# Attention and expert feed-forward on one core: softmax denominators of pairs 8 to 28 from one sum of eight tiles, and two moved VectorE steps

## The reference

```python
attn = jnp.einsum('bhnd,bhsd->bhns', q, k) * scale      # scale = 64 ** -0.5
attn = jnp.clip(attn, -11.0, 11.0)
attn = jax.nn.softmax(attn, axis=-1)                    # over the 1024 context rows
out = jnp.einsum('bhns,bhsd->bhnd', attn, v)
out = out.transpose(0, 2, 1, 3).reshape(b, n, INNER)
return out @ Wo + bo
...
sel = jax.nn.sigmoid(jnp.einsum('bsd,ed->bse', input_tensor, expert_sel))
scores = jax.nn.relu(jnp.einsum('bsd,edh->bseh', input_tensor, keys))
out = jnp.einsum('bseh,ehv,bse->bsv', scores, values, sel)
```

## Time and profile before

| | |
|---|---|
| median of 3 runs | 1008.09 us (1007.96 to 1010.86) |
| profiled execution, its own time | 1009.1 us |
| its span, first to last instruction | 1007.3 us |
| TensorE busy | 978.5 us, 97% |
| VectorE busy | 809.4 us, 80% |
| ScalarE busy | 532.1 us, 53% |
| DMA share of 16 engines | 32.4% |

### The profile page before, as it was taken

The page is one execution under the profiler, slowest core; times in us unless marked ns, Lnnn a source line. Parts: engine busy times, 40 slices in busy tenths (PEclk is TensorE's granted clock), DMA queues, the critical chain, the costliest instruction groups (busy, mean ns, idle before and its releaser), DMA issues. The chain is left out here.

```text
span 1007.3 us, 16017 instructions
## 1 busy us (share of the span) xinstructions
PE 978.5 (97%) x5712; PEld 621.8 (62%) x5712; DVE 809.4 (80%) x1275; ACT 532.1 (53%) x765; POOL 146.5 (15%) x130
## 2 busy tenths in 40 slices
PE   4999999999999999999999999998999989999998
PEld 3755555555555555555555555554555468888898
DVE  7888999999899989998889888988889876545322
ACT  3666666666566656565656555555555542222221
POOL 3200000000000000000000000320000144445443
PEclk9999999999999999999999999999999999999999
DMA  7343333323232333233322223232222471242331
GB/s 215 114 133 96 112 92 112 120 75 91 74 90 74 93 89 104 75 96 84 96 80 86 64 85 84 84 85 84 85 64 66 136 272 61 109 127 85 125 105 42
DMA packets 68601, 99.84 MB, mean 99 GB/s; under 512 B 21872, under 2 KB 44656, under 8 KB 66480
## 3 DMA queue, kind: packets, MB, share of 16 engines
q1 hardware_dynamic: 68528, 98.89, 32.4%
HBM read 70.01 MB, written 10.75 MB: 80 GB/s over the span
## 5 line engine op out<-in xcount | busy, mean ns | idle before, releaser
L1130 ACT ACTIVATE wide_a<-score_ps 128x1024 f32<-128x1024 f32 x256 | 248.8, 1026 | 118.2 <-PE score_ps L886 118.0
L1433 DVE TENSOR_SCALAR wide_a<-wide_a 128x1024 f32<-128x1024 f32 x256 | 169.9, 691 | 44.1 <-ACT wide_a L1130 44.0
L1442 DVE TENSOR_TENSOR p_sum<-wide_a 128x1024 f32<-128x1024 f32 x128 | 158.0, 1234 | 2.3
L899 PE MATMUL o_ps<-wide_a,v_sb 128*64 128x512 f32 x512 | 124.0, 605 | 0.8 <-issue 0.8
L899 PE MATMUL o_ps<-wide_a,values_a 128*64 128x512 f32 x512 | 124.0, 605 | 0.2 <-issue 0.2
L886 PEld LDWEIGHTS score_ps<-q_hi,k_hi 64*128 64x128 f32 x512 | 47.9, 183 | 111.4 <-issue 77.5
L886 PE MATMUL score_ps<-q_hi,k_hi 64*128 64x512 f32 x512 | 114.6, 444 | 1.7 <-DVE k_lo L1426 0.9
L1961 DVE SCALAR_TENSOR_TENSOR act<-h_ps,wide_a 128x512 f32<-128x512 f32 x62 | 42.8, 690 | 87.5 <-PE h_ps L152 82.1
L1885 ACT CAST act_hi<-act 128x512 fp32r<-128x512 f32 x64 | 39.8, 621 | 138.4 <-DVE act L1961 138.4
L886 PE MATMUL score_ps<-q_hi,k_lo 64*128 64x512 f32 x512 | 101.0, 391 | 0.0
L886 PE MATMUL score_ps<-q_lo,k_hi 64*128 64x512 f32 x512 | 100.5, 389 | 0.0
(11 more groups left out here) (225 smaller groups left out, 1929.6 us busy)
## 6 DMA issues: line engine op xcount, KB each, us to landing
wide_a<-sel_dram SPq DMA_DIRECT2D x16, 1024.0 KB, 4.6
k_swap<-k SPq DMA_DIRECT2D x124, 128.0 KB, 2.3
w_hi<-packs_hi SPq DMA_DIRECT2D x26, 384.0 KB, 3.0
w_lo<-packs_lo SPq DMA_DIRECT2D x26, 384.0 KB, 3.6
den<-inv_dram SPq DMA_DIRECT2D x64, 128.0 KB, 2.8
ctx_raw<-ctx SPq DMA_DIRECT2D x24, 128.0 KB, 2.2
packs_hi<-w_hi SPq DMA_DIRECT2D x8, 384.0 KB, 3.0
packs_lo<-w_lo SPq DMA_DIRECT2D x8, 384.0 KB, 3.6
```

The costliest lines, as they stand in the source:

```text
L899: mm = pe.matmul(o_ps[DH * h:DH * h + DH, :], v_sb[n // 2 % 2][:, at:at + DH], probs[s % RING][:, h, :], start=(s == 0), stop=(s == STEPS ...
L1130: act.activation(probs[s % RING][:], score_ps[s % 2][:], ACT.Exp, scale=DH ** -0.5).then_inc(exp_done, 1)
L1433: dve.tensor_scalar(probs[s % RING][:], probs[s % RING][:], CLIP_HI, CLIP_LO, ALU.min, ALU.max).then_inc(clipped, 1)
L1442: dve.tensor_tensor(p_sum[m][:], first, second, ALU.add).then_inc(summed_up, 1)
```

## The change

Three things, all in the attention.

1. For n in `EIGHTS` (8 to 28, 21 pairs) VectorE makes one sum of all eight tiles. `sum_quad(n, 0)` stays; new is `sum_six(n)`, which adds `p_sum[1]` into `p_sum[2]` at the end of macro step 3; `sum_all(n)` adds `p_sum[2]` into `p_sum[3]` where `sum_quad(n, 1)` stood. TensorE's four matmuls with ones then take 256 columns each instead of 512, head h and query half e at partition 64h+32e. ScalarE copies 256 columns of `den`, each turning DMA moves half, and VectorE inverts without adding first.
2. The output remainder `split_o(n-2)` of pairs 9 to 28 moves from behind `sum_up` and `stats` in macro step 0 to directly behind the first two clips.
3. `normalize` of the context tile (n below 22) moves from ahead of clip 2 to behind it.

```diff
--- before.py
+++ after.py
@@ -50,6 +50,7 @@
 CLIP_LO = 1.670170079024566e-05
 
 FIRST_TILES = 10
+EIGHTS = range(PAIRS, NPAIR - 3)
 FIRST_DUOS = FIRST_TILES // 2
 MACROS = STEPS // 2
 QUAD = 32
@@ -191,16 +192,23 @@
     for h in range(2):
         for e in range(2):
             at = DH * h + QUAD * e
-            row = sh.den[at:at + 1, :].rearrange("a (p j) -> a p j", p=DH)
-            sp.dma_start(sh.den_rows[DH * h:DH * h + DH, e, :], row).then_inc(sh.den_turned, DMA)
+            if n in EIGHTS:
+                row = sh.den[at:at + 1, 0:NQ // 2].rearrange("a (p j) -> a p j", p=QUAD)
+                sp.dma_start(sh.den_rows[at:at + QUAD, 0, :], row).then_inc(sh.den_turned, DMA)
+            else:
+                row = sh.den[at:at + 1, :].rearrange("a (p j) -> a p j", p=DH)
+                sp.dma_start(sh.den_rows[DH * h:DH * h + DH, e, :], row).then_inc(sh.den_turned, DMA)
 
 
 def invert_den(dve, sh, n):
 
     wait(dve, sh.den_turned, 4 * DMA * (n + 1))
     wait(dve, sh.inv_stored, DMA * n)
+    if n in EIGHTS:
+        dve.reciprocal(sh.inv_rows[:], sh.den_rows[:, 0, :]).then_inc(sh.den_inv, 1)
+        return
     dve.tensor_tensor(sh.inv_rows[:], sh.den_rows[:, 0, :], sh.den_rows[:, 1, :], ALU.add).then_inc(sh.den_added, 1)
-    wait(dve, sh.den_added, n + 1)
+    wait(dve, sh.den_added, n + 1 - sum(1 for i in EIGHTS if i < n))
     dve.reciprocal(sh.inv_rows[:], sh.inv_rows[:]).then_inc(sh.den_inv, 1)
 
 
@@ -508,7 +516,7 @@
 
         def quads(n):
 
-            return sum(1 if i in THREE_PARTS else 2 for i in range(min(n, NPAIR - 2) + 1))
+            return sum(1 if i in THREE_PARTS else 3 if i in EIGHTS else 2 for i in range(min(n, NPAIR - 2) + 1))
 
         def k_half(t, half):
 
@@ -916,7 +924,13 @@
                 pe.wait_ge(ones_ready, 1)
                 wait(pe, den_evac, n)
                 wait(pe, y_added, 2 * (n - 1) - (1 if n >= NPAIR - 2 else 0))
-                if n == NPAIR - 1:
+                if n in EIGHTS:
+                    for e in range(2):
+                        for h in range(2):
+                            at, half = DH * h + QUAD * e, slice(e * (NQ // 2), (e + 1) * (NQ // 2))
+                            mm = pe.matmul(side_ps[at:at + QUAD, 0:NQ // 2], ones[:], p_sum[3][:, h, half],
+                                           start=True, stop=True)
+                elif n == NPAIR - 1:
                     mm = ones_round([(0, p_sum[2]), (1, p_sum[3])], False, True)
                 elif n in THREE_PARTS:
                     ones_round([(0, p_sum[1])], True, False)
@@ -1138,7 +1152,8 @@
                 act.wait_ge(den_ready, n + 1)
 
                 wait(act, o_scaled, n)
-                act.copy(den[:], side_ps[:]).then_inc(den_evac, 1)
+                width = NQ // 2 if n in EIGHTS else NQ
+                act.copy(den[:, 0:width], side_ps[:, 0:width]).then_inc(den_evac, 1)
 
             def round_weights(w):
 
@@ -1447,6 +1462,17 @@
                 first, second = p_sum[2 * half], p_sum[2 * half + 1]
                 dve.tensor_tensor(second[:], first[:], second[:], ALU.add).then_inc(quads_up, 1)
 
+            def sum_six(n):
+
+                dve.wait_ge(quads_up, quads(n) - 2)
+                dve.wait_ge(summed_up, MACROS * n + 4)
+                dve.tensor_tensor(p_sum[2][:], p_sum[1][:], p_sum[2][:], ALU.add).then_inc(quads_up, 1)
+
+            def sum_all(n):
+
+                dve.wait_ge(quads_up, quads(n) - 1)
+                dve.tensor_tensor(p_sum[3][:], p_sum[2][:], p_sum[3][:], ALU.add).then_inc(quads_up, 1)
+
             dve.wait_ge(power_ready, 3)
             stats_first(0)
             stats_first(1)
@@ -1515,14 +1541,14 @@
                 p, t = n + 1, n + FIRST_TILES
                 for m in range(MACROS):
                     last = n == NPAIR - 1
-                    if m == 1 and t < TILES:
-                        wait(dve, turned, t - FIRST_TILES)
-                        normalize(t, ctx_n[:], x_n[:])
                     if m == 3 and n in (24, 25):
                         head_rows(2 * (n - 24))
                     if m == 3 and n in (26, 27):
                         head_split_x(2 * (n - 26))
                     clip(n, 2 * m)
+                    if m == 1 and t < TILES:
+                        wait(dve, turned, t - FIRST_TILES)
+                        normalize(t, ctx_n[:], x_n[:])
                     if n == 0 and m == 0:
                         rope_first_cos(1)
                     if m == 1 and p < NPAIR:
@@ -1532,12 +1558,15 @@
                         scale_o(dve, sh, n - 1)
                     if n == 0 and m == 0:
                         rope_first_sin(1)
-                    if m == 0 and n >= NPAIR - 3:
+                    if m == 0 and n > PAIRS:
                         split_o(dve, sh, n - 2, n % 2)
                     if m == 0 and n >= 3:
                         add_y(dve, sh, n - 3, 1, job_ps[1] if last else side_ps, bo)
                     if m == 0 and n > 0 and n - 1 not in THREE_PARTS:
-                        sum_quad(n - 1, 1)
+                        if n - 1 in EIGHTS:
+                            sum_all(n - 1)
+                        else:
+                            sum_quad(n - 1, 1)
                     if m == 2 and n >= 2:
                         add_y(dve, sh, n - 2, 0, side_ps, bo)
                     sum_up(n, m)
@@ -1548,7 +1577,7 @@
                             stats(t)
                         if n == 0:
                             split_v_weights(1)
-                        if 2 <= n < NPAIR - 3:
+                        if 2 <= n <= PAIRS:
                             split_o(dve, sh, n - 2, n % 2)
                         if n == 29:
                             invert_gate(dve, sh, 0, 0)
@@ -1574,6 +1603,8 @@
                         add_y(dve, sh, n - 2, 1, job_ps[0], bo)
                         split_o(dve, sh, n - 1, 0)
                         split_keys(3)
+                    if m == 3 and n in EIGHTS:
+                        sum_six(n)
                     if m == 3:
                         if t < TILES:
                             split_tile(t)
```

## The result

The changed kernel takes **1015.88 us** (median of 4 runs, 1014.43 to 1016.45); the kernel before took 1009.05 beside it (4 runs). The ratio is 1.0072, with a 95% interval from 1.0046 to 1.0098. It is slower by some 7 us where I had forecast 6.8 us faster, and the time lies outside my range. The profiled execution took 1014.43 us, its span 1012.6, against 1007.3 before.

A forecast was written before the change was run, and what follows sets the result against it. TensorE, busy 97% of the span, was taken as the bound. Narrow blocks gain 9.0 us, less 1.2 of stalls and 1.0 in pair 27: 6.8 us, so 1008.1 to 1001.3 us, range 998.6 to 1005.3.

The forecast's parts named there:

- The matmuls with ones: TensorE's block with ones at half width: 1.00 to 0.57 us, 0.43 per pair, 9.0 us over 21 pairs.
- The rule that I weighed: Narrow weight loads set the block's pace: 0.87 us, a gain of 0.13 each; as a rival 1006.4 us, chance 6%.
- What VectorE gets: VectorE's extra 128x1024 sum, 1.14 us, less the half-sums' addition, 0.19: net 0.95 us per pair, 20 us in all.
- my sign of 0.6: Rival 1 decides where more than 0.6 us of VectorE idle stays in a pair with x rows.
- rival 1: VectorE becomes the bound, the ring of waits not opened: pairs last 25.3 or 25.0 us, kernel 1028 us; chance 6%.
- The ring: ScalarE and VectorE wait for each other before exponential 2; early `o_lo` opens it, clip 2 at 334.0 instead of 334.75.
- The deadline: TensorE's ones need `sum_all` 7.14 us into a pair; odd pairs 9 to 21 stall about 1.2 us in all.
- At nothing, the DMAs: Turning DMAs, still four with half the bytes, cost nothing: hidden behind the inverse, which VectorE comes to only later.
- `normalize` for pairs 0 to 7: Moving the normalizing there was put at nothing, since TensorE's few waits are not on it.
- From pair 22 on: No tile is left to normalize, so VectorE keeps more of the idle time it is given back; no size given.
- Pair 27, late by 1.0 us: The last sum, 0.79 us ahead of the ones before, gets 1.74 more and makes TensorE wait about 1.0 us.
- Rival 2: TensorE waits for `sum_all` in nearly every pair, 0.1 to 0.4 us; half the 9.0 goes: 1004.5 us; chance 14%.

The follow-up runs named there:

- free_narrow: Kernel before with the narrow block with ones in pairs 8 to 28, no extra VectorE sum (tiles 0 to 3 left out of denominators): 999.54 us, ratio 0.9929.
- after_swap: Changed kernel with the sum of the first four tiles' pairs put ahead of the scaling of o_raw: 1006.81 us, ratio 0.9993.
- norm_only: Kernel before with only `normalize` moved behind clip 2, in all pairs that have a tile: ratio 1.0039.
- olo_only: Kernel before with only the output remainder `split_o` early in pairs 9 to 28: ratio 1.0021.
- sums_only: Kernel before with the sums of eight and narrow blocks in pairs 8 to 28, but neither move: 1017.38 us, ratio 1.0087.
- single mends: Changed kernel with one repair: old normalizing place up to pair 8 (1.0027), `split_o` behind the last sum (1.0016), or sums of eight only to pair 23 (1.003).
- three_mends: Changed kernel with normalizing in its old place up to pair 8, sums of eight only to pair 23, `split_o` behind the last sum: 1008.94 us, ratio 1.0003.
- olo_behind_sum: Changed kernel with the output remainder `split_o` directly behind the last sum of eight instead of ahead of it: ratio 1.0016.
- the exchange: Sum of the first four tiles' pairs put ahead of the scaling of o_raw; made alone in the kernel before: 1005.99 us, ratio 0.9971.
- mends_swap: `three_mends` with the sum of the first four tiles' pairs put ahead of the scaling of o_raw: 999.21 us, ratio 0.9908.
- before_swap: Kernel before with only the sum of the first four tiles' pairs put ahead of the scaling of o_raw: 1005.99 us, ratio 0.9971.
- sums_to_23: Changed kernel with one sum of eight only for pairs 8 to 23; pairs 24 to 28 sum in fours again: ratio 1.003.
- norm_late_pairs: Changed kernel with the normalizing back ahead of clip 2 in pairs 0 to 8: ratio 1.0027.

## Why the prediction was wrong

- **The matmuls with ones, 0.43 us each: right.** 1.00 to 0.57 us, 0.42 per pair in `free_narrow`. All eight loads of a block start within 0.1 us. The line of the narrow block in pair 12 (ns of one, then the first and last start in us):

```profile
L931 PEld LDWEIGHTS side_ps<-p_sum,ones x8: 106/108/109, 334.9 to 335.0; 128*32 128x32 f32 x8
L931 PE MATMUL side_ps<-p_sum,ones x8: 379/391/403, 334.9 to 335.2; 128*32 128x256 f32 x8
```

The rule that I weighed (the Trainium skill, TensorEngine Tiling, section Restrictions: column tiling disables fast weight load) gives no time; 0.87 was my estimate, eight loads of 108 ns one after another. The trace, with 0.57, shows that the loads don't set the pace here.

- **What VectorE gets, 0.95 us per pair: right** (345.34 to 359.47 us over 16 pairs is 0.88). In pair 12 it is busy for 23.02 us, less than the 23.31 that I had, which is why its 0.89 us of idle there, over my sign of 0.6 for rival 1, did no harm.
- **The ring is opened: right.** Clip 2 is at 337.58, 9.78 us into pair 12; I had said 9.8.
- **The deadline, 1.2 us of stalls in pairs 9 to 21: wrong, and the central fault.** They were 4.3. I had the last sum of pair 13 at 7.05 us into the pair (it ended at 7.0) and that of pair 11 at 7.6 or 7.7 (7.8). But I took three pairs as the sample, and let even pairs recover 1.1 us. Pair 12 ended at 6.8, not 6.0, and pairs 14, 18 and 20 at 7.2 to 7.7. ("Three lie as late as 11" was misread as well: before the change the last sum ended at 5.96 us in pair 11, 5.88 in 15 and at most 5.62 in the other odd ones.) The margin of 0.1 us was below the size of what VectorE waits for behind DMAs: 2.9 us in 8 waits for `den`, all in pairs 9 to 20, and 4.5 in 5 for `k_swap`, of which 1.3 lie ahead of pair 22. Six of the eight stalls (pairs 11, 15, 17, 19, 20, 21) have a wait for `den` in the pair before them; the wait of 1.07 us for `k_swap` in pair 13 stands ahead of that of 14. In `after_swap`, where the last sum no longer waits for `den`, it ends in pairs 11, 17 and 19 at 7.0 to 7.1 instead of 7.4 to 7.9. Over pairs 9 to 24 of the changed kernel:

```profile
DVE wide_a L1448 <- ACT wide_a L1144: 12.9, 16, 1.9
DVE k L1409 <- DMA k_swap<-k: 4.5, 5, 1.6
DVE o_raw L233 <- DMA den<-inv_dram: 2.9, 8, 0.5
```

- **At nothing, the DMAs, "hidden behind the inverse, which VectorE comes to only later": only half looked at.** Halving the turning DMAs cost nothing, but the DMAs that follow the inverse were hidden by idle time that I was spending in the same text; no term stood for them. One such wait stands late in pair 18, two sums ahead of the last sum, which falls in pair 19; there TensorE waits 0.76 us ahead of the ones:

```profile
494.29 0.69 DVE L233 TENSOR_TENSOR o_raw<-o_raw,den 128x512 f32<-128x512 f32 x1 [0.51 <-DMA den<-inv_dram]
494.89 1.22 DVE L1463 TENSOR_TENSOR p_sum<-p_sum 128x1024 f32<-128x1024 f32 x1
```

- **At nothing, "`normalize` for pairs 0 to 7": wrong, 3.5 us.** The cover that I named (TensorE's few waits are not on it) was never checked against the late `o_lo` of these pairs. A step that moves from inside a wait to behind it is new work on the path there; its price was 0.3 to 0.6 us a pair in pairs 4 to 6 and nothing in 7 and 8, where there was room. In pair 3 it was 1.8, because the inverse came later as well and VectorE waited 1.23 us for `den` in pair 2: the same DMA that I had put at nothing.
- **From pair 22 on, "VectorE keeps more of what it is given back": wrong for 25 and 26, 4.6 us.** No tile is normalized there, but the head statistics and the new sum stand together ahead of the last sum, and the clock falls behind one of the two waits (pair 26).
- **Pair 27, late by 1.0 us:** TensorE waited 2.74 us ahead of the block. The pair still came out 0.5 us shorter, against the 0.6 longer that I had (1.0 less a block), but that is luck: the stall of 2.75 us at the key projection stands in the profile of the kernel before and in none of the 17 others. Against kernels without the extra sum (25.3 us in `norm_only`, 25.6 in `olo_only`) pair 27 is 2.5 to 2.9 us longer.

```profile
703.34 0.84 PE L931 MATMUL side_ps<-p_sum,ones 128*32 128x256 f32 x8 [2.74 <-DVE p_sum L1474]
```

Set against my sum of 6.8, by stage: pairs 2 to 8 took 3.5 us; pairs 9 to 24 gave 1.9 where I had 6.9 - 1.2, 3.8 short (3.1 of it in waits); pairs 25 and 26 took 4.6 where two blocks were to give 0.86, 5.5 short; pair 27 was better than forecast by 1.1; all after it fell short by 0.4. That is 12.1, and 6.8 - 12.1 is -5.3, the span's 5.3 us. Rival 2, which named waits in nearly every pair, had the mechanism, but with a floor at half the gain. No rival had the other stages, and rival 1 (VectorE as the bound, the ring not opened) did not occur here: VectorE still idles 1.1 us in pair 11. It is `sums_only`, without the moves, that shows its ring.

What stays open: why the late DMA comes when it does, and how much of each cause there is in the time, since the single mends take 4 to 6 us each from the changed kernel, 14 in all, and together (`three_mends`) only 7. It was not tried to make the inverse's chain itself shorter, nor to move the head statistics alone.

## What to carry to other kernels

An engine's idle time is a cover for every wait that now falls into it; before spending it, list those waits (from the trace, for that engine and the whole stage, not three pairs) and put steps that need no DMA ahead of those that do. A moved step must be costed in each stage where it is moved: the same place can be inside a wait in one and behind it in another. And a margin of a tenth of a microsecond on an engine that works in order is no margin.

## What was not expected of the hardware

- Now and then the inverse's chain of DMAs lands about 2 us late: VectorE waited 2.3 us in `three_mends` (pair 10) and 1.9 in `norm_only` and `olo_behind_sum` (pair 18 in both), against at most 1.0 in the other pairs from 9 to 24 of the kernels without the exchange. In pair 2 a wait of 1.5 to 2.0 us is the rule there.
- `three_mends` lay between 1004.68 and 1014.35 us in 12 runs, `mends_swap` between 997.7 and 1000.78 in 6; `before_swap` lay between 1004.09 and 1007.09 in 10, the kernel before in the same lot between 1005.19 and 1013.3 in 28. That the exchange narrows the scatter is not shown, though: `after_swap` has it and lay between 1003.73 and 1010.92 in 10.
- A wait of TensorE can cost more than itself, and its length doesn't tell whether it will. Behind the five waits of 2.6 to 3.0 us from pair 9 to 27 in all profiles (two of them 2.74: pair 27 of the changed kernel, pair 11 of `three_mends`) the granted clock was 1.2 GHz for a while; pair 11 of `three_mends` was 4.3 us longer than in `mends_swap`. Below that it went either way. The clock fell behind 1.77 us (pair 26 of the changed kernel), 1.79 and 2.18 (pairs 25 and 27 of `olo_behind_sum`) and 1.84 (pair 3 of `sums_to_23`). It stayed at 2.4 GHz behind 1.79 (pair 26 of `norm_late_pairs`), 1.99 (pair 25 of the changed kernel), 2.10 (pair 19 of `olo_behind_sum`) and 2.54 (pair 25 of `after_swap`), and behind every wait under 1 us. What decides it is open.
